# A vision tower in one kernel: one activation table set for logarithm and exponential on ScalarE

## The reference

```
h = h + L0_attn(layernorm(h))   # a scan over the 38 tokens, 16 states per feature
h = h + L0_ffn(layernorm(h))    # top 2 of 8 experts, 192 -> 768 -> 192 with gelu
h = h + L1_attn(layernorm(h))   # down to 96, a selective scan forward and one backward, up to 192
h = h + L1_ffn(layernorm(h))    # top 2 of 8 linear experts
```

```
dt = softplus(dt @ dt_W + dt_b)          # log(1 + exp(x))
h  = exp(dt * A) * h + (dt * u) * B ;  y = (h * C).sum + u * D ;  y = y * silu(z)
```

## Time and profile before

| | |
|---|---|
| three runs, median (lowest to highest) | 1078.17 us (1074.69 to 1086.61) |
| the profiled execution, its own time | 1080.07 us |
| its span on the core | 1078.3 us |
| TensorE busy | 738.6 us, 68% |
| VectorE busy | 653.5 us, 61% |
| POOL busy | 442.8 us, 41% |
| ScalarE busy | 428.5 us, 40%, 862 instructions |
| DMA | 168.95 MB, mean 157 GB/s |

### The profile page before, as it was taken

The page is one execution under the profiler, slowest core; times in us unless marked ns, Lnnn a source line. Parts: engine busy times, 40 slices in busy tenths (PEclk is TensorE's granted clock), DMA queues, the critical chain, the costliest instruction groups (busy, mean ns, idle before and its releaser), DMA issues.

```text
span 1078.3 us, 10771 instructions
## 1 busy us (share of the span) xinstructions
PE 738.6 (68%) x3238; PEld 561.6 (52%) x3238; DVE 653.5 (61%) x954; ACT 428.5 (40%) x862; POOL 442.8 (41%) x304
## 2 busy tenths in 40 slices
PE   3847768668355539999927268577778587865845
PEld 2535546446234329999915146455556455543623
DVE  3157997798698231111110589789877987799330
ACT  1546447147131113333304355573726372644120
POOL 0045653764786230110120155454457435645503
PEclk9888879779566559999967568797969896976857
DMA  9674552632642048999810767676585658576102
GB/s 352 285 192 114 133 157 65 167 92 78 152 116 52 22 130 260 292 286 290 244 35 0 179 175 194 159 197 176 135 226 141 184 134 228 140 188 188 30 7 72
DMA packets 79581, 168.95 MB, mean 157 GB/s; under 512 B 12052, under 2 KB 30240, under 8 KB 78768
## 3 DMA queue, kind: packets, MB, share of 16 engines
q1 hardware_dynamic: 75040, 161.86, 54.6%
q0 software_dynamic: 4496, 6.55, 2.1%
HBM read 148.33 MB, written 20.01 MB: 156 GB/s over the span
## 4 chain that ended last, share of the span: by engine, by line
PE 39%; DVE 20%; issue 13%; POOL 10%; ACT 8%; DMA 7%; SPq 2%; DVEq 0%; POOLq 0%; ACTq 0%
PE PS L1504 39%; DVE ST L1192 5%; POOL dA L655 3%; DMA BB<-rows_d 3%; DVE BB L1178 3%; POOL slots_d L669 3%; POOL PR L664 2%; POOL PR L723 1%; DMA xp<-slots_d 1%; DMA CR<-c 1%; DMA keep_d<-KEEP 1%; DVE BB L1164 1%; ACT L817 1%; ACT aP L886 1%; ACT L886 1%
## 5 line engine op out<-in xcount | busy, mean ns | idle before, releaser
L1504 PE MATMUL PS<-PR,CM 128*128 128x304 f32 (+1 forms) x768 | 225.0, 439 | 132.4 <-POOL PR L723 74.8
L1504 PEld LDWEIGHTS PS<-PR,CM 128*128 128x128 f32 x768 | 154.5, 238 | 188.8 <-POOL PR L723 92.0
L1192 DVE TENSOR_TENSOR_SCAN ST<-dA,BB 128x608 f32<-128x608 f32 x96 | 160.2, 1673 | 4.4 <-POOL PR L723 4.2
L867 ACT ACTIVATE dA<-dA,negA 128x304 f32<-128x304 f32 x192 | 93.7, 539 | 145.8 <-DMA BB<-rows_d 145.6
L723 POOL TENSOR_TENSOR PR<-ST,q_V 128x608 f32<-128x608 f32 x48 | 75.1, 1565 | 134.7 <-DVE ST L1192 122.9
L723 POOL TENSOR_TENSOR PR<-ST,p_V 128x608 f32<-128x608 f32 x48 | 86.1, 1798 | 102.0 <-DVE ST L1192 94.3
L655 POOL TENSOR_TENSOR dA<-dA,aP 128x608 f32<-128x608 f32 x48 | 87.4, 1820 | 72.5 <-DMA BB<-rows_d 60.7
L1169 DVE TENSOR_TENSOR_SCAN ST<-dA,BB 128x608 f32<-128x608 f32 x48 | 98.7, 2056 | 17.8 <-issue 16.4
L1178 DVE TENSOR_TENSOR BB<-BB,PS 128x608 f32<-128x608 f32 x96 | 74.0, 773 | 29.0 <-DMA BB<-rows_d 28.3
L957 ACT ACTIVATE HID<-PS,WX 128x128 f32<-128x128 f32 x162 | 47.6, 365 | 108.0 <-PE PS L1504 108.0
L699 POOL DMA_DIRECT2D outs_d<-xp x27 | 14.6, 543 | 135.6 <-DVE xp L1364 135.6
(11 more groups left out here) (331 smaller groups left out, 1400.0 us busy)
## 6 DMA issues: line engine op xcount, KB each, us to landing
dA<-rows_d SPq DMA_DIRECT2D x144, 304.0 KB, 3.8
BB<-rows_d SPq DMA_DIRECT2D x144, 304.0 KB, 4.4
WX<-ex_m SPq DMA_DIRECT2D x27, 576.0 KB, 4.8
WX<-ex_m SPq DMA_DIRECT2D x27, 387.0 KB, 4.3
slots_d<-WXR SPq DMA_DIRECT2D x8, 960.0 KB, 27.7
WXR<-ex_r SPq DMA_DIRECT2D x27, 192.0 KB, 5.6
WX<-gates_d SPq DMA_DIRECT2D x4, 1216.0 KB, 6.1
CM<-c SPq DMA_DIRECT2D x1, 4430.0 KB, 20.1
```

What stands on the lines that cost most here:

```text
L867: last = nc.scalar.activation(dAq[:, slot, i, :], dAq[:, slot, i, :], ACT.Exp, scale=negA[:, j:j + 1])
L1192: nc.vector.tensor_tensor_scan(flat(STq[:, c % 2], back), flat(dAq[:, slot], back), flat(BBq[:, slot], back), 0.0, ALU.mult, ALU.add).then ...
L1504: return nc.tensor.matmul(out, lhsT, rhs, start=first, stop=last)
```

## The change

With it the program has 43 table loads in place of 86. The core of the diff (the call stands in the same way ahead of the other Ln and Exp, and the clearing ahead of the other Silu, Sigmoid and Gelu):

```diff
+LN_AND_EXP = 6
...
         @block.scalar
         def _(act):
+            tables = [None]
+
+            def ln_and_exp():
+
+                if tables[0] != LN_AND_EXP:
+                    tables[0] = LN_AND_EXP
+                    act.add_instruction(mybir.InstLoadActFuncSet(name=nc.get_next_instruction_name(), engine=mybir.EngineType.Activation,
+                                                                 act_func_set_id=LN_AND_EXP))
+
+            ln_and_exp()
             act.wait_ge(s_const[0], 64)
             act.wait_ge(prep_pool, 1)
+            ln_and_exp()
             nc.scalar.activation(dt0[:, :], cm("log_dt"), ACT.Exp)
...
             def log_of(s, rows, bank, log):
 
+                ln_and_exp()
                 nc.scalar.activation(s.VE[0:rows, :], PS[0:rows, bank, 0:T], ACT.Ln, bias=eps_col[0:rows, :]).then_inc(log.sem, 1)
 
             def power_of(s, rows, log, rstd, g, k):
                 act.wait_ge(log.sem, log.after(g, k))
+                ln_and_exp()
                 nc.scalar.activation(s.RS[0:rows, :], s.VE[0:rows, :], ACT.Exp, scale=-0.5).then_inc(rstd.sem, 1)
...
                 act.wait_ge(landed[slot].sem, landed[slot].after(g, 32 * landings(k, c)))
                 for i in range(QB):
                     j = k * FEAT_BLOCKS + c * QB + i
+                    ln_and_exp()
                     last = nc.scalar.activation(dAq[:, slot, i, :], dAq[:, slot, i, :], ACT.Exp, scale=negA[:, j:j + 1])
...
+                tables[0] = None
                 nc.scalar.activation(s.ZS, PS[:, Z_BANK, 0:PK], ACT.Silu)
```

4 lines of the change are left out of this document (added).

## The result

Four runs of the changed kernel took 1066.34 us in the median (1065.4 to 1067.34), four of the kernel before 1080.73 us (1074.69 to 1086.61): a ratio of 0.9881, 95% interval 0.9851 to 0.9911. Forecast were 1068.1 us and a gain of 12.0. The same kernel, measured twice more beside the experiments, gave 0.9928 (0.9904 to 0.9951) and 0.9890 (0.9858 to 0.9922). The mean of the three is 0.9900, some 10.8 us. So the time met the forecast, but two of its terms gave next to nothing, and gains that the forecast did not have stood in for them.

A forecast was written before the change was run, and what follows sets the result against it. ScalarE was no bottleneck by its sum (8% of the chain; TensorE 39%, VectorE 20%), so only loads others waited for count. 7.8 + 3.1 + 1.1 = 12.0 us off 1080.07 gave 1068.1 us, range 1059 to 1076.

The forecast's parts named there:

- Rival 2: A removed load gives its row and as much again, by a drain or overlap: 19.8 us, 1060.3 us; chance 0.06.
- Six bare places: At 29, 364, 590, 682, 1022 and 1035 us nothing runs beside; one load each gives 1.30 us, together 7.8.
- 632 and 724 us, 3.1 us: Second-pass places: VectorE's waits plus half of a stretched operation at each, 3.1 us, bounds 1.4 and 4.8.
- these are the sure parts, 1.39 together: At 632 and 724 us VectorE's waits of 0.81 and 0.58 us were counted as certain gain.
- between 0 and 1.68 I take half: At 632 and 724 us line 1244 may escape POOL's product, saving up to 1.68 us; 0.84 counted at each.
- 231 and 307 us, 1.1 us: First-pass places where VectorE waited 1.25 and 1.01 us for the exponential, taking turns with POOL; 1.1 us counted.
- between 0 and 2.26 us I take half: At 231 and 307 us half of VectorE's waits was counted, 1.1 us, since POOL does not move.
- Twelve other places at nothing: One after the experts, two first-pass, nine second-pass; eleven hidden by VectorE's own queue, one net nothing: 0 us.
- Moved waits at nothing: Explicit loads now stand behind their functions' waits, in four sorts of place: cost 0 to 2 us, taken 0.
- Place (a): First load after the experts now waits for the variance: 1.28 us exposed, the second load's 1.30 gone, net nothing.
- Rival 1: Only places without parallel work pay; VectorE and POOL's pattern swallows the rest: 6.5 us, 1073.6 us; chance 0.18.
- Rivals 3 and 4: Kept loads of the new set take longer, so slower; or automatic loads still follow, leaving 1080 us; chance 0.03 each.

The follow-up runs named there:

- rest_only: Changed kernel with the loads put back at the six places where nothing else runs, the other 31 still gone (55 loads): 1079.16 us, ratio 1.0008.
- all_undone: Changed kernel with all 86 loads again, the put-back ones explicit and kept behind their waits: 1079.42 us, ratio 1.0015 to the kernel before.
- after: The changed kernel, first measurement and trace, against the kernel before: 1066.34 us, ratio 0.9881.
- after_again: The changed kernel, same file, measured and traced a second time against the kernel before: 1069.67 us, ratio 0.9928.
- after_third: The changed kernel, same file, measured and traced a third time against the kernel before: 1067.84 us, ratio 0.9890.
- four_more: Changed kernel with four extra table loads at each of five places where nothing else runs: 1098.55 us against 1081.73 before.
- cover_four: Changed kernel with four extra loads ahead of the step size's logarithm at four covered second-pass places (16 loads): 1076.62 us, ratio 0.9956 to the kernel before.
- bare_only: Kernel before with the change only at the six places where nothing else runs (12 loads gone, 74 left): 1071.27 us, ratio 0.9935.
- ahead: Changed kernel with its kept shared-set loads moved ahead of their waits and behind the last Silu, Sigmoid or Gelu: 1067.61 us, ratio 0.9865 to the kernel before.
- ahead_again: The kernel of ahead measured again, beside the changed kernel: 1066.86 us, ratio 0.9877 to the kernel before.
- both kernels with the narrow product: POOL's second-pass product cut to 8 of 304 columns, other products left out: with all 86 loads 1054.0 us, with loads only at six places 1045.88 us.

## Why the prediction was right, and where it was not

- **The price, 1.30 us for each load on the chain: right.** 1.27 to 1.28 us at four bare places, 1.42 at 682 us (where VectorE's idle time was 1.63 and is now 0.21), and 5.15 for four in a row. Rival 2 falls, with the drain.
- **Six bare places, 7.8 us: right.** The table gives 1.27 + 1.27 + 1.42 + 1.28 + 1.28 = 6.5 for five. The first has 1.28 between its logarithm and its exponential, once the 1.10 us ahead of the logarithm are taken off its 2.37 (the clock, below): 7.8. Alone they measured 0.9935, 7.0 us.
- **632 and 724 us, 3.1 us: wrong, it was nothing.** The step that failed is "these are the sure parts, 1.39 together", and "between 0 and 1.68 I take half" with it. The idle time of VectorE was no lower bound of the gain: VectorE arrives earlier in a pattern that POOL sets, and meets its product in another operation. The table shows it for both: with the loads gone 632 us gives -1.42 to -0.22 us and 724 us -0.80 to 0.39, and either place does as much with its loads standing. To start first does not protect an operation either: the one at 633.86 starts 0.33 us ahead of POOL's product and takes 2.31 us, that at 624.29 starts 0.43 us ahead and takes 2.41, while POOL's take 1.48 and 1.47.
- **231 and 307 us, 1.1 us: wrong, 0.2.** The step is "between 0 and 2.26 us I take half". VectorE got its 1.3 and 1.1 us and gave back all but 0.2 within three operations. The sentence ahead of that step, that POOL does not move when ScalarE is quicker, was right, and it should have set the value, not a bound.
- **Twelve other places at nothing: right** (rest_only, 1.0008). **Moved waits at nothing: right, as far as the time can tell** (all_undone, 1.0015). Place (a), net nothing: -0.01 us in every trace.
- **Rival 1** named the mechanism, that the pattern swallows everything, and its 6.5 us were 1.3 short as the place at 682 us did give. 7.8 us off the profiled 1080.07 would have been 1072.3. **Rivals 3 and 4** fall with 43 loads at 1,283 ns.
- **So why did the time still meet 1068.1?** By luck. Nearly all of the forecast's 4.2 us for the shared places were missing, and after the bare places 3 us of the mean 10.8 came from elsewhere. The traces put them at the start (1.4 to 2.6 us up to 227 us beside the load, by the first two rows of the table) and in the stretches from 372 to 591 us, where no gain came from a removed load (chance, as all_undone shows). Of the start 0.5 to 0.8 us go with the first load, by way of the clock, which the forecast had only as 3 us of either sign; the rest stays open. The shown waits at 231, 307 and 632 us did vanish as forecast, and proved nothing.
- Of the marks: from 556 to 593 us the lead grew by 2.5 instead of 1.3, the rest being 1.2 from the clock at 580 us; from 1017 us on by 3.2 instead of 2.6; ScalarE is busy for 372.9 us, as said.

## What to carry to other kernels

Count a removed instruction at its full row only where nothing else runs beside the chain; there it comes out to the hundredth of a microsecond. Where the waiting engine shares something with a third one that keeps its own time, idle time that names the removed work is the most it can give, not the least, and it is safest to count it at nothing. Look also whether the chain that ended last leads through that idle time at all: at 231 and 307 us it did not. Ask of each engine in such a pattern who moves when the work is earlier; if one does not, look for the operation that will meet it next. An engine's busy time that rises without one more operation is the mark of it.

## What the runs showed of the hardware

**The clock at the start.** The first stage and a stretch in it in the kernel before, and the same two in the changed one (from:to, length, busy us of PE, PEld, DVE, ACT, POOL, granted clock, DMA share, GB/s):

```profile
20.00:70.00 50.00, 33.64 (x120) 23.33 (x118) 10.34 (x21) 20.64 (x36) 3.65 (x3) 0.84 0.73 270
...
31.77:50.73 18.96, 17.84 (x64) 13.05 (x65) 0.46 (x3) 9.51 (x19) 0.00 (x0) 0.87 0.71 297
```

```profile
20.00:66.40 46.40, 31.83 (x120) 22.32 (x118) 10.28 (x21) 18.09 (x34) 3.59 (x3) 0.90 0.78 291
...
29.29:47.64 18.35, 17.23 (x64) 12.64 (x65) 0.46 (x3) 9.53 (x19) 0.00 (x0) 0.91 0.88 368
```

Two pairs of matmuls at 26 us, before and after:

```profile
26.63 1.38 PE L1504 MATMUL PS<-p_RS,ones_d 128*128 128x304 f32 x2 [1.53 <-ACT p_SQr L773]
27.80 1.22 PE L1504 MATMUL PS<-p_SQr,ones_d 128*128 128x304 f32 x2
```

```profile
26.53 0.78 PE L1536 MATMUL PS<-p_RS,ones_d 128*128 128x304 f32 x2 [1.53 <-ACT p_SQr L787]
27.15 0.68 PE L1536 MATMUL PS<-p_SQr,ones_d 128*128 128x304 f32 x2
```

From 26 to 28 us the granted clock is 0.62 in the kernel before and 1.00 in the changed one: the second pair runs at TensorE's lower level (1.2 GHz) before and still at the higher (2.4 GHz) in the changed kernel, after the same work and the same gap of 1.53 us. That is 1.1 us. The second pair took 0.67 or 0.68 us in after, after_again, after_third, four_more and cover_four, and 1.22 in the kernel before, all_undone, rest_only, bare_only, ahead, ahead_again and both kernels with the narrow product. The first load that was on the chain stood behind these matmuls, at 29.59 us, so it can't have slowed them. The hidden one at 26.59 us ran beside them, but bare_only and ahead don't have it there: they have ScalarE's instructions of the changed kernel up to there, and the slower pair. Whether the change has a part in it stays open.

The stretch behind the normalization is clearer. From 31.77 to 50.73 us of the kernel before TensorE does the same 64 matmuls in every kernel. The lead grows there by 0.48 to 0.79 us in the seven traces in which ScalarE goes from the first logarithm to the exponential without a load (after, after_again, after_third, bare_only, cover_four, ahead and ahead_again), at a granted clock of 0.90 or 0.91. It grows by -0.33 to 0.03 in the five others, one load there or four, at 0.85 to 0.87, as in the kernel before. So this gain goes with the removed load; it is a second one, beside the load's own 1.28 us. Why TensorE is back at its higher level sooner no run shows.

From 569 to 591 us, ahead of the first step size, the granted clock was 0.77 before and 0.82 in all_undone, which gained 1.39 us there without one load less.

**The experts.** The stretch from 372 to 556 us, in which no load was touched, differs by up to 6.3 us between traces (-2.21 to 4.06). That is half of what the change was to bring, so a single pair of traces says nothing by its spans; the growth of the lead place by place does.
